# Softmax sums of three causal attentions: inverted as 128x8 over a trip through memory instead of as 128x512 in a bank of PSUM

## The reference

```
s = softmax(mask(Q K^T) / 8) V Wo        # layers 0, 1, 3: causal, 16 heads of 64
                                         # layer 0: rotary, 4 key heads; layer 3: one key head
                                         # and a "null" key that is the same for all queries
s = layernorm(x + attention over 64x64 feature pairs)   # layer 2, 8 heads
g = routed experts (layers 0, 3), routed and shared experts (1), a four-matrix gated net (2)
```

## Time and profile before

| | us |
|---|---|
| three runs | 2008.48, 2005.79, 2002.66 (median 2005.79) |
| the profiled execution | 2003.36 |
| its span in the profile | 2001.0 |
| PE / DVE / POOL / ACT busy | 1849.8 / 1399.3 / 1225.7 / 964.6 |

### The profile page before, as it was taken

The page is one execution under the profiler, slowest core; times in us unless marked ns, Lnnn a source line. Parts: engine busy times, 40 slices in busy tenths (PEclk is TensorE's granted clock), DMA queues, the critical chain, the costliest instruction groups (busy, mean ns, idle before and its releaser), DMA issues.

```text
span 2001.0 us, 31764 instructions
## 1 busy us (share of the span) xinstructions
PE 1849.8 (92%) x9960; PEld 1272.3 (64%) x9960; DVE 1399.3 (70%) x3825; ACT 964.6 (48%) x2008; POOL 1225.7 (61%) x1600
## 2 busy tenths in 40 slices
PE   5999999999895999999999999998999999899985
PEld 4566666666694666666676567887556665455554
DVE  8898888888344776766666456455788888776733
ACT  2544445545454455455455435444444444455443
POOL 1766788888553566776777700012467676799744
PEclk8999999999997899999999999999899999999998
DMA  5224233322344334344344120001322222222243
GB/s 149 67 70 114 68 94 95 79 57 60 89 142 114 84 84 98 86 110 95 88 101 98 42 88 22 1 13 30 82 57 57 65 68 60 65 77 70 56 117 98
DMA packets 125968, 155.57 MB, mean 78 GB/s; under 512 B 21880, under 2 KB 66200, under 8 KB 125544
## 3 DMA queue, kind: packets, MB, share of 16 engines
q1 hardware_dynamic: 121704, 145.42, 29.5%
q0 software_dynamic: 4096, 8.12, 1.2%
HBM read 47.84 MB, written 17.40 MB: 33 GB/s over the span
## 4 chain that ended last, share of the span: by engine, by line
PE 60%; DVE 14%; POOL 9%; issue 8%; ACT 3%; DMA 3%; SPq 3%; POOLq 0%; DVEq 0%; ACTq 0%
PE P L858 59%; POOL acc L1639 3%; POOL yd L1656 3%; DVE mx L2019 2%; DVE P L2030 2%; SPq L1760 1%; POOL acc L1636 1%; DMA qA<-hq 1%; POOL pr L1617 1%; POOL xg L1647 1%; DVE rd L2078 1%; DVE P L2077 1%; DVE z L2084 1%; PE P L957 1%; DVE mx L2040 0%
## 5 line engine op out<-in xcount | busy, mean ns | idle before, releaser
L1639 POOL TENSOR_TENSOR acc<-acc,pr 128x512 f32<-128x512 f32 (+3 forms) x768 | 677.3, 904 | 87.3 <-ACT pr L1398 63.0
L1398 ACT ACTIVATE pr<-P 128x512 f32<-128x512 f32 (+1 forms) x768 | 396.9, 568 | 331.4 <-PE P L858 288.0
L858 PE MATMUL P<-qA,kA 128*128 128x512 f32 (+2 forms) x1024 | 392.9, 387 | 17.1 <-ACT pr L1398 11.1
L858 PE MATMUL P<-pr,vt 128*64 128x512 f32 (+3 forms) x2304 | 403.3, 491 | 4.7 <-POOL pr L1617 4.5
L858 PE MATMUL P<-qB,kB 128*128 128x512 f32 (+2 forms) x1024 | 367.8, 365 | 0.0
L858 PE MATMUL P<-kA,qA 128*128 128x512 f32 (+2 forms) x1152 | 318.2, 376 | 30.5 <-DMA qA<-hq 9.3
L1617 POOL TENSOR_SCALAR_AFFINE_SELECT pr<-pr 128x256 f32<-128x256 f32 x384 | 156.5, 408 | 272.6 <-ACT pr L1398 215.7
L858 PEld LDWEIGHTS P<-pr,vt 128*64 128x64 f32 x2304 | 155.2, 137 | 217.3 <-issue 178.7
L2019 DVE TENSOR_REDUCE mx<-P 128x1 f32<-128x512 f32 x384 | 241.6, 683 | 30.8 <-PE P L858 29.0
L858 PEld LDWEIGHTS P<-qA,kA 128*128 128x128 f32 x1024 | 195.1, 191 | 102.8 <-ACT pr L1398 48.5
L858 PEld LDWEIGHTS P<-kA,qA 128*128 128x128 f32 x1152 | 193.7, 195 | 102.1 <-issue 25.8
(11 more groups left out here) (350 smaller groups left out, 2766.0 us busy)
## 6 DMA issues: line engine op xcount, KB each, us to landing
qA<-hq SPq DMA_DIRECT2D x384, 128.0 KB
kA<-stage SPq DMA_DIRECT2D x158, 128.0 KB, 2.3
qB<-qB SPq DMA_DIRECT2D x96, 128.0 KB, 2.5
kB<-stage SPq DMA_DIRECT2D x79, 128.0 KB
nr<-null_share SPq DMA_DIRECT2D x64, 128.0 KB, 3.0
yd<-in_c_zero SPq DMA_DIRECT2D x32, 128.0 KB, 2.7
w<-in_L_W SPq DMA_DIRECT2D x16, 256.0 KB, 5.0
xg<-xg SPq DMA_DIRECT2D x24, 129.0 KB
```

The source lines that it names most:

```text
L858: return P.matmul(out, lhs, rhs, start=start, stop=stop)
L1398: S.activation(a.pr[slot][:, r, 512 - wide:512], m.bank[b][:, 512 - wide:512], AF.Exp, scale=0.125).then_inc(s.free[b], 1)
L1639: G.tensor_tensor(acc[:, sl], acc[:, sl], pt[:, sl], ALU.add).then_inc(s.acc, 1)
```

## The change

- **Sums.** ACT copies the close bank to `rd` at once (*close*), which frees the bank. SPq folds two of its 128 partitions (one for each head) into `rc`, 128x8 (*fold*); DVE takes the reciprocal there (*recip*; in the third attention after adding the null share, now also 128x8); SPq writes it to `sum_share` in memory (*spread*) and reads it back as 128x512, each head's row for 64 partitions (*cast*, tile `rb`).
- **Product.** ACT copies the pv bank to `z` without the factor (*zraw*), and POOL multiplies `z` by `rb` (*div*). The old way stays for the last pair (b, p) = (1, 7) of each attention (`at_end`), two chunks of 32.
- **Adds.** One POOL instruction adds both heads of a tile.
- **Buffers.** In the first attention `rb` has one buffer, which lies in the router's `xg` rows, in the others two. The values of the second attention have two buffers instead of three.
- **Order.** The three strings of `STEPS` are new. `'` now moves an item a job back. Per job they have 7, 16 and 15 `+` where there were 7, 14 and 18.

```diff
+    0: ("k0 S k0' q0 R1 S q0' q1 F1 S S C1 k0\" q1' q0\" V1 + + Z1 q1\" k1 F0 S + W0 + v1 M0 B0 S C0 I1 W1 M1 S "
+        "M2 v0 S I0 M4 k1' k1\" O0' S D0 M6 + Z0 M5 S R0 + V2 M3 S B1 D1 M7 + V1 M8 S M9 O1"),
+    1: ("S q0 q0' S + k0 q1 R1 k0' + F1 S q0\" S k0\" C1 I1 V1 Z1 + q1' S + v0 q1\" S M1 + W1 M0 S O0' M2 S v1 "
+        "M3 S + M5 D1 B1 k1' F0 k1 + k1\" C0 + V3 + R0 S M6 + + I0 + W0 M4 V V M8 S S + D0 M9 + O1 B0 Z0 + + "
+        "M7"),
+    3: ("q0 + + q0' S V4 k0' + k0 k1 k0\" R1 S q0\" F1 v1 V4 C1 k1' + + S S + M2 M0 S q1' q1 S k1\" + q1\" M1 + "
+        "V2 S I1 + W1 + M3 Z1 S + M5 + B1 v0 D1 S M6 F0 C0 + R0 + S M9 W0 M4 V4 + I0 M8 O0' S B0 Z0 S D0 M7 "
+        "O1")}
...
-                if kind in HELD and len(got) == n - 1:
+                if kind in HELD and len(got) == n - 1 and (kind != "close" or at_end(*item[2:4])):
...
-                if at >= 3:
-                    w.wait_ge(s.pv, od.nth("pv", L, (at - 3) // 4, 2 * ((at - 3) % 4) + 1, 1, 7))
+                if at >= 2:
+                    w.wait_ge(s.pv, od.nth("pv", L, (at - 2) // 4, 2 * ((at - 2) % 4) + 1, 1, 7))
...
+            elif kind == "close" and not at_end(*k[1:3]):
+                a, old = m.A[k[0]], pl.close_before(*k)
+                w.wait_ge(s.full[b], f)
+                if old:
+                    w.wait_ge(s.fold, 16 * od.nth("fold", *old))
+                S.copy(a.rd[:], ps[:]).then_inc(s.free[b], 1)
+            elif kind == "zraw":
...
+                w.wait_ge(s.pv, od.nth("pv", L, bb, p, c, kts(L, c)[-1]))
...
+                S.copy(a.z[pl.chunk(*k) % 4][:], m.bank[b][:]).then_inc(s.free[b], 1)
...
-                        G.tensor_tensor(acc[:, sl], acc[:, sl], pt[:, sl], ALU.add).then_inc(s.acc, 1)
+                    G.tensor_tensor(acc[:, :, sl], acc[:, :, sl], pt[:, :, sl], ALU.add).then_inc(s.acc, 1)
+            elif kind == "div" and not at_end(*k[1:3]):
...
+                w.wait_ge(*pl.emptied("pv", *k, 0))
+                w.wait_ge(s.cast, 16 * od.nth("cast", *k))
+                G.tensor_tensor(z[:], z[:], a.rb[n], ALU.mult).then_inc(s.div, 1)
...
+                    Y.dma_start(m.A[3].nl[i % 4][:], src).then_inc(s.n_in[i % 2], 16)
...
+            elif kind == "fold":
...
+                w.wait_ge(*pl.emptied("close", *k))
...
+                Y.dma_start(a.rc[n], a.rd[0:128:64, :].rearrange("r (p e) -> r p e", e=8)).then_inc(s.fold, 16)
+            elif kind == "spread":
...
+                w.wait_ge(s.recip, od.nth("recip", *k))
...
+                Y.dma_start(sd[pl.chunk(*k)].rearrange("(p e) -> p e", e=8), m.A[k[0]].rc[n]).then_inc(s.spread, 16)
+            elif kind == "cast":
...
+                w.wait_ge(s.spread, 16 * od.nth("spread", *k))
...
+                if old:
+                    w.wait_ge(*pl.weighed(*old))
+                src = sd[pl.chunk(*k)].rearrange("(r n) -> r n", r=2).unsqueeze(1).broadcast_to([2, 64, 512])
+                Y.dma_start(a.rb[n], src).then_inc(s.cast, 16)
...
+            elif kind == "recip":
...
+                w.wait_ge(s.fold, 16 * od.nth("fold", *k))
+                if L == 3:
+                    w.wait_ge(s.n_in[n], 16 * (i // 2 + 1))
+                    chain(V.tensor_tensor(a.rc[n], a.rc[n], a.nl[i % 4][:], ALU.add))
+                V.reciprocal(a.rc[n], a.rc[n]).then_inc(s.recip, 1)
```

More of the change, by code:

```diff
@@ L196 @@
 SCORED = [(0, kt) for kt in range(4)] + [(1, kt) for kt in range(8)]
+SHARES_OUT = {"C": "close", "F": "fold", "I": "recip", "W": "spread", "B": "cast", "Z": "zraw", "D": "div", "O": "out"}
 STEPS = {
[L200 to L205, removed]
+    0: ("k0 S k0' q0 R1 S q0' q1 F1 S S C1 k0\" q1' q0\" V1 + + Z1 q1\" k1 F0 S + W0 + v1 M0 B0 S C0 I1 W1 M1 S "
[6 more added lines that the diff above has]
+        "O1")}
 def project(L, kind, b, p, c):
@@ L265, in step @@
         n = int(what[1:].strip("'\"")) if len(what) > 1 else 0
-        done = (L, *jobs[j - n], n) if j - n >= 0 else None
+        at = j - n - what.count("'")
+        done = (L, *jobs[at], n) if 0 <= at < 16 else None
         if what[0] == "v":
@@ L289, in step, with finish @@
                     od.add("nrd", L, *jobs[at], n)
[L290 to L294, removed]
-            od.add("div", *done)
[L296 to L300, removed]
+        elif what[0] in SHARES_OUT and done:
+            finish(SHARES_OUT[what[0]], done)
+    def finish(kind, done):
+        b, p = done[1:3]
+        if kind == "out":
+            if p % 2:
+                if done == (3, 0, 1, 0):
+                    od.add("nbias", 3)
+                od.add("out", *done)
+        elif not at_end(b, p):
+            od.add(kind, *done)
+        elif kind == "close":
+            od.extend([(x,) + done for x in ("close", "dsum", "yinv") if L == 3 or x != "dsum"])
+        elif kind == "div":
+            od.add("div", *done)
     scored = []
@@ L334, in attention_order @@
     od.extend([("pv", *k) for k in scored])
-    od.extend([(k, L, 1, 7, 1) for k in ("close", "dsum", "div", "out") if L == 3 or k != "dsum"])
+    left = [(L, *jobs[j], c) for j in range(13, 16) for c in range(2)]
+    for kind in SHARES_OUT.values():
+        for done in left:
+            if (kind,) + done not in od.place:
+                finish(kind, done)
     for items in behind:
@@ L716, in signals @@
     s.w_hi, s.root, s.xn_a, s.x_hi = one("w_hi"), one("root"), one("xn_a"), one("x_hi")
-    s.q_hi, s.k_hi, s.inv = one("q_hi"), one("k_hi"), one("inv")
+    s.q_hi, s.k_hi, s.inv, s.recip, s.div = one("q_hi"), one("k_hi"), one("inv"), one("recip"), one("div")
+    s.fold, s.spread, s.cast = one("fold"), one("spread"), one("cast")
     s.rt_wh, s.rt_exp, s.xs, s.c_act, s.silu = one("rt_wh"), one("rt_exp"), one("xs"), one("c_act"), one("silu")
@@ L759, in __init__ @@
                 self.normed |= {(it[1], g): n for g in range(lo // 4, hi // 4)}
+        self.casts = [it[1:] for it in od.items if it[0] == "cast"]
+        self.closes = [it[1:] for it in od.items if it[0] == "close"]
+        self.n_div = {}
+        for it in od.items:
+            if it[0] == "div" and not at_end(*it[2:4]):
+                self.n_div[it[1:]] = len(self.n_div) + 1
         self.adds, n = {}, 0
```

117 lines of the change are left out of this document (80 added, 37 removed).

## The result

The changed kernel takes **2151.4 us** (median of four runs, 2138.77 to 2158.6) where the one before takes 2004.85 (2002.66 to 2008.48): a ratio of 1.0725, 95% interval 1.0696 to 1.0755. It is 7.25% slower. The forecast was 1982 us, with a range up to 2085; the measured time lies outside both. The profiled execution took 2158.6.

The account below looks back on a forecast made before the run. PE was taken to bound the first two attentions, a DVE and ACT series, then POOL, the third. Gains of 9 + 3 + 9 - 1 + 2 = 22 us from 2003.36 gave 1981 to 1984, forecast 1982 us, range 1955 to 2085.

Parts of the forecast that it names:

- the new path: Close to product: 2.3 to 3.0 us per DMA, some 10.5 in all; 1 us a job booked where POOL is nearly full.
- rival 1: Two DMA engines carry the cast, 6 to 9 us more each; about 2105 us in full, 2080 said; chance 0.23.
- DVE: Instructions dropped per chunk: 3.7 us less a job in the first two attentions, about 5 less in the third.
- ACT: Ln and Exp (1.23 us) become two copies out of PSUM (1.2 us); zero either way.
- POOL: Ten adds a job saved (1.9 us), two products added (2.56 us): 0.5 us more a job.
- SPq: Three more issues a chunk, 3.6 us a job (2.4 in the third attention); no cost while no wait precedes a query copy.
- Merged adds: POOL's adds for both heads in one instruction: 186 ns fixed cost saved each, 1.9 us a job.
- Third attention: DVE and ACT series leaves the chain: 9 us gained in six bisection jobs, 3 in the first two, 9 in later ones.
- Rival 3: DVE's two-input instructions wait for POOL's longer adds, 62 us on DVE in the third attention: 1988 us; chance 0.13.

Follow-up runs that it names:

- experiment 5: Kernel before, its null-share load (`nr`) as one DMA with two rows outermost instead of two DMAs of 64 partitions: 2013.97 us, ratio 1.0018.
- experiment 1: Changed kernel, each cast cut by rows into two DMAs of 64 partitions, 64 outermost: 2004.48 us, ratio 0.9971 to the kernel before.
- experiment 2: Changed kernel, each cast cut by columns into two DMAs of 256 columns, both with two rows outermost: 2227.58 us, ratio 1.11 to the kernel before.
- experiment 3: Kernel before plus 20 separate 256 KB DMAs behind its end: 7.09, 4.70, 3.54, 3.02, 3.47 us each for 2, 4, 8, 16, 1 rows outermost.
- experiment 9: Changed kernel, cast cut by rows, new path and merged adds in the third attention only, the others as before: 1990.63 us, ratio 0.9928 to the kernel before.
- experiment 11: Changed kernel, cast cut by rows, new path everywhere, adds per head in the first two attentions: 2012.16 us, ratio 1.0024 to the kernel before.
- experiment 4: Changed kernel, cast cut by rows, the fold also in two DMAs, one for each head: 2020.42 us, ratio 1.0048 to the kernel before.
- experiment 6: Kernel before, with only the adds merged, one POOL instruction for both heads: 2007.49 us, ratio 0.9981.
- experiment 8: Changed kernel, cast cut by rows, new path in the third attention only, merged adds in all three: 2001.06 us, ratio 0.9957 to the kernel before.
- experiment 10: Changed kernel, cast cut by rows, new path in the third attention only, adds per head in all three: 1998.88 us, ratio 0.9967 to the kernel before.

## Why the prediction was wrong

**The step that failed** is the cast in *the new path*: "for each DMA the nearest row is nr's 3.0 us". `nr` was the nearest row in bytes and purpose, but it is written as two DMAs, each with 64 partitions outermost (the minus lines of experiment 5), while the cast has the two heads outermost. The prediction saw the shape and made it rival 1, at 0.23, against which it held that "the copies now land in 2 to 3 us"; those copies have other outermost dimensions and said nothing on it. Experiments 1, 2 and 3 show the rival to be the mechanism: 147 of the 147 us. In place of 2.3 to 3.0 us the cast took 7.7 from issue to product. The rival's landing time was about right: 8.5 us by the queue's rate, 6.9 to 7.6 by itself. The chance was not: the shape could be read in the diff, the Trainium skill stated the rule, and no row spoke against it.

**Rival 1 was priced too low**, 103 us in full, and three quarters of that (77) for the figure given. Between the traces of the changed kernel and of experiment 1 lie 86.3 us in the first attention (62 forecast), 31.8 in the second (21) and 23.9 in the third (20), 6 elsewhere. Two terms:
- The early jobs of the first attention. The rival let POOL alone be late, which costs little where POOL has slack: 12 us for six jobs. From 116.63 to 346.63 six jobs take 230.0 us, 38.4 more than before. There POOL waits 40.5 us for casts and PE in turn 15 for the product (2.9 and 1.4 us in experiment 1, six jobs of 31.6 us). What queues behind a cast is delayed in the other two attentions: in the second, 6 folds that DVE waits for were issued while a cast was under way and took 5.2 to 8.0 us to the reciprocal, the others 1.9 to 2.8; PE waits 19.6 us for query copies (10.4 in experiment 1). Most of DVE's 72.9 us for folds is not the cast's, since experiment 1 keeps 55.7 of them. The prediction had a sentence for query copies behind a cast and no number.
- PE's clock. Its busy time rose from 1849.8 to 1903.3 us for the same 9960 matmuls, while the mean granted clock went from 0.973 to 0.947: a mean between its two levels, 1.2 and 2.4 GHz, with more of the span at the lower one than before. With the cast mended both are back (1851.4 us, 0.972). In the changed kernel's windows it is 1.00 in the second attention, 0.94 in the first and 0.91 in the first's six jobs, where the waits are longest. So 54 us of PE's time beside 156 between the two spans are matmuls that ran longer, not waits; how many of the 54 lie on the path wasn't worked out.

**With the cast mended**, was the forecast of 22 us right? No: experiment 1 gives about 6 (ratio 0.9971). Its profiled execution, 2010.52, lies 6 us above its own median; the stretch to the second attention may be where, by the scatter shown above. Against the kernel before, with the forecast behind each:

| stage | experiment 1 | forecast | experiment 9 |
|---|---|---|---|
| first attention, from its third job | +5.6 | +1 | -1.4 (old path) |
| to the second (6 us of scatter) | +7.5 | 0 | +2.4 |
| second attention | +3.8 | -2 | -1.3 (old path) |
| to the third | +2.1 | 0 | +1.0 |
| third, first two jobs | +2.1 | -3 | +1.6 |
| third, the rest | -15.0 | -18 | -15.3 |
| tail | +2.3 | 0 | +2.1 |

- *DVE*: 3.7 us a job forecast; in the first attention 23.6 became 139.77/7 = 20.0 with experiment 1's jobs (300.40 to 510.28). Right. In the third 5 forecast, 4.5 measured.
- *ACT*: zero either way. Right.
- *POOL*: +0.5 forecast, +1.0 measured (184.70/7 = 26.4 against 25.3). The merged add took the 2.38 us forecast, and the product 1.28. The saving was mis-sized: two adds in a row overlap in the records, 361.9/288 = 1.26 us of busy time for each of 1.28, so that merging saves 0.13 us, not 0.19: 1.3 us a job, not 1.9.
- *The new path*: with the fast cast its cover of 10 us suffices (9 us of waits in all), so the +1 us a job booked for it was not a wait. The loss in the first attention lies where POOL is nearly full: the last seven jobs lose 7.3 us (5 forecast), the six before them gain 1.7 (4 forecast), and the windows of experiment 11 show how the seven follow POOL's work.
- *SPq* "no cost": probably wrong. In experiment 4, 90 issues more came with 16 us; the change adds 240 and the cast by rows another 90. The count was misread too: the kernel before issues 10 to 29 a job in the first attention, not 12 to 20, and 24 in the second, where experiment 1 has 29 to 33. What part of the second attention's +3.8 is theirs wasn't tried by itself.
- *Merged adds*: the prediction gave them only gains. With the old path they cost some 4 us in the first attention, counted from its first job (459.3 us in experiment 6, 459.6 in 8; 455.5 and 455.7 in the kernel before, 454.0 in 9), and they give 4 to 5 in the third. That an add now waits for both heads' exponentials, where the first head's half could go ahead, would explain the cost; this was argued and not tried.
- *Third attention*: right in mechanism. The six links are off the chain, the six jobs beside the bisection take 29.8 us (1507.93 to 1686.94), forecast 29.3: 5.7 us of the 9 forecast. Those behind it, with fewer scatters each, give the 9 forecast for them; experiment 10, without merged adds, gives 5.5 there. The first two jobs lost 2 us where 3 were to be gained.
- *Rival 3* (62 us on DVE) did not come. The maxima of a chunk take two instructions with two SBUF inputs, one behind the other. Experiment 9, with merged adds, then experiment 10, with adds per head, DVE by form:

```profile
L2134 DVE TENSOR_TENSOR mx<-mx,sn 128x8 fp32r<-128x8 f32 x32 | 28.4, 887 | 1.1
...
L2135 DVE TENSOR_TENSOR mx<-sn,mx 128x8 f32<-128x8 f32 x32 | 9.4, 294 | 1.1
```

```profile
L2134 DVE TENSOR_TENSOR mx<-mx,sn 128x8 fp32r<-128x8 f32 x32 | 16.2, 507 | 1.1
...
L2135 DVE TENSOR_TENSOR mx<-sn,mx 128x8 f32<-128x8 f32 x32 | 14.3, 446 | 1.1
```

The first of the pair is longer beside the longer adds, the second shorter: 1.18 us together against 0.95, and 1.31 in the kernel before, whose adds are the short ones. The 30 null adds take 550 and 475 ns. So the doubling that the prediction reckoned with is not there. ACT waits for the pair (78.8 us in experiment 9, 71.0 in experiment 10, 119.1 before), and it makes 0.9% of the chain in 1500:1668, under 2 us. The Trainium skill, page "SBUF — State Buffer", section "Who interferes with whom", has such an instruction contend with a GpSimd instruction that reads SBUF; instructions of 128x8 that take between 0.17 and 2.3 us agree with that, and these runs don't show that the waits grow with the length of GpSimd's adds.

## What to carry to other kernels

Read the outermost dimension of every DMA that a change adds, and of the row that prices it: 256 KB with two rows outermost took 7 us by itself and 7.7 in the kernel up to its reader, the same bytes cut into one DMA a row 3.7, and the slow one also delays what stands behind it. Where a diff shows a shape and no row speaks against the rule, the rule is the forecast and not the rival. And a change that helps one stage may be tried stage by stage: the new path and the merged adds, kept to the third attention, gave 0.72%, everywhere, with the cast mended too, only 0.3%.

## What the runs showed that was not expected

- A transfer confined to two engines delays others: in the changed kernel the fold, 4 KB, lands in time for the reciprocal to start 2.0 us after its issue at 1005.21, but takes 6.1 us when it is issued (1018.08) while a cast is under way. In experiment 1 the folds that DVE waits for take 1.9 to 2.4 us.
- More and smaller packets made the confined cast dearer: 75 us for 90 casts, with the bytes unchanged (experiment 2).
- A stage can differ by 6 us between two executions of one kernel, while the one before it agrees within 0.2 (the stretch behind the first attention): a second trace of the kernel before tells which differences mean something.
- Waits came with a lower clock of PE: 54 us more of matmul time, in a kernel whose cause touches no matmul, and gone again with the cast mended.
- Whether merging two POOL instructions gains has turned its sign with the engine's load: +3.5 us in six jobs with 23.6 us of POOL's work in 31.9 (141.84 us), nothing in the seven with 25.3 in 28.9, -8.1 in the seven with 27.8 in 31.1.
